# Near scores of the second attention in f16 halves, and an earlier signal for part of the last gathers

## The reference, cut to what matters

```
I = jnp.where(local[None], jnp.inf, I)
_, idx = jax.lax.top_k(I, kk)                       # kk = 96: 64 near, 32 chosen
...
scores = (jnp.einsum('bhld,bhlkd->bhlk', q_c, k_c) + jnp.einsum('bhld,blkd->bhlk', q_r, key_r)) * scale
attn = jax.nn.softmax(scores.astype(jnp.float32), axis=-1)
out = jnp.einsum('bhlk,bhlkd->bhld', attn, v)
```

## Time and profile before

| | us |
|---|---|
| median of 3 runs | 2271.33 |
| lowest, highest | 2270.91, 2275.74 |
| the profiled execution, its own time | 2271.51 |
| its span, first to last instruction | 2269.9 |
| PE, DVE, ACT, POOL busy in the span | 2103.8, 1787.5, 1732.0, 1830.0 |

### The profile page before, as it was taken

How to read it: one execution, slowest core, us unless ns; L and a number is a source line. 1 busy time by engine, 2 the same in 40 slices (tenths; PEclk the granted TensorE clock), 3 DMA queues, 4 the chain that set the end, 5 groups by cost and what they waited for, 6 DMA issues and landing times. The chain is left out here.

```text
span 2269.9 us, 56900 instructions
## 1 busy us (share of the span) xinstructions
PE 2103.8 (93%) x22674; PEld 1261.6 (56%) x22674; DVE 1787.5 (79%) x3457; ACT 1732.0 (76%) x3507; POOL 1830.0 (81%) x1239
## 2 busy tenths in 40 slices
PE   5899999999999999999999979977989889987888
PEld 1466666666666666666666646642445444444444
DVE  7788888888888888888888558978878896887314
ACT  5898898898989988989989935657567775775543
POOL 4899999999999999999999935627777777777720
PEclk9999999999999999999999989978599997998779
DMA  4000000000000000000000000111211111111101
GB/s 152 1 2 2 2 2 2 2 2 2 2 2 2 2 2 2 2 2 2 2 2 2 2 15 23 39 40 27 52 37 32 39 37 34 38 31 36 38 9 37
DMA packets 44688, 43.19 MB, mean 19 GB/s; under 512 B 21312, under 2 KB 33424, under 8 KB 44176
## 3 DMA queue, kind: packets, MB, share of 16 engines
q1 hardware_dynamic: 28560, 23.35, 3.6%
q0 software_dynamic: 15872, 16.28, 3.2%
HBM read 33.83 MB, written 1.57 MB: 16 GB/s over the span
## 5 line engine op out<-in xcount | busy, mean ns | idle before, releaser
L380 POOL TENSOR_TENSOR probs_lo<-probs,probs_hi 128x1024 f16<-128x1024 f32 x512 | 1076.9, 2130 | 42.9 <-ACT probs L430 42.4
L494 DVE TENSOR_REDUCE part_max<-aux 128x1 f32<-128x512 f32 x1024 | 677.6, 686 | 91.2 <-PE aux L568 86.8
L429 ACT ACTIVATE probs_hi<-scores 128x512 f16<-128x512 f32 x1024 | 630.2, 615 | 134.6 <-PE scores L601 117.8
L430 ACT ACTIVATE probs<-scores 128x512 f32<-128x512 f32 x1024 | 636.6, 622 | 0.0
L1617 POOL DMA_INDIRECT far<-key_table,placeT x456 | 452.2, 992 | 142.9 <-issue 138.7
L617 PE MATMUL acc<-v,probs_hi 128*128 128x65 f16 x4096 | 451.1, 193 | 2.3 <-POOL probs_lo L380 2.3
L619 PE MATMUL acc<-v,probs_hi 128*128 128x64 f16 x4096 | 452.2, 195 | 0.0
L621 PE MATMUL acc<-v,probs_lo 128*128 128x65 f16 x4096 | 450.6, 192 | 0.0
L617 PEld LDWEIGHTS acc<-v,probs_hi 128*128 128x128 f16 x4096 | 382.5, 96 | 82.6 <-POOL probs_lo L380 2.5
L619 PEld LDWEIGHTS acc<-v,probs_hi 128*128 128x128 f16 x4096 | 380.0, 97 | 75.5
L568 PE MATMUL aux<-k_a,q_a 128*128 128x512 f16 x1024 | 392.1, 383 | 5.2 <-DVE roped L480 2.1
(11 more groups left out here) (329 smaller groups left out, 3939.7 us busy)
## 6 DMA issues: line engine op xcount, KB each, us to landing
far<-key_table,placeT POOLq DMA_INDIRECT x496, 2.4
qT<-qT SPq DMA_DIRECT2D x16, 256.0 KB
e_w<-in_e_w SPq DMA_DIRECT2D x48, 64.0 KB, 1.9
x<-in_x SPq DMA_DIRECT2D x4, 256.0 KB, 3.8
cos<-in_cos SPq DMA_DIRECT2D x1, 1024.0 KB, 6.8
sin<-in_sin SPq DMA_DIRECT2D x1, 1024.0 KB, 8.8
e_w<-in_e_w SPq DMA_DIRECT2D x2, 512.0 KB, 4.0
out<-x SPq DMA_DIRECT2D x4, 256.0 KB, 2.7
```

The lines of the kernel that those rows point to most:

```text
L380: pool.tensor_tensor(probs_lo[:, slot], probs[:, wide], probs_hi[:, slot], ALU.subtract).then_inc(low_ready, 1)
L429: act.activation(probs_hi[:, slot, i], bank, ACT.Exp, scale=float(DH0) ** -0.5)
L430: act.activation(probs[:, wide, i], bank, ACT.Exp, scale=float(DH0) ** -0.5).then_inc(probs_ready, 1)
L494: dve.tensor_reduce(part_max[g % 2][:, n % QT, n // QT:n // QT + 1], bank, AX.X, ALU.max).then_inc(aux_free, 1)
```

## The change

It has two parts.

**Near scores in f16.** The near keys are kept as an f16 high part on all 128 partitions (the same 64 rows twice, `near_hi`) and an f16 low part on 64 (`near_lo`). For that each near job makes four f32 matmuls with the identity more, which put the second copy on the upper partitions, and DVE subtracts the high part after ACT's copy. The queries for the near keys are kept as high part over low part on 128 partitions (`near_qT`); ACT writes the high part and DVE the low part, with one subtraction for each of "q" 2 and 3 in each tile. The turn bank is then free when DVE is done and not when ACT is. The score is one f16 matmul of 128 partitions (high and low queries with high keys) and one of 64 (high queries with low keys), 256 columns each, in place of the f32 one. The far queries keep their form, in a tensor of their own.

**The last tile's gathers.** Its gathers 16 to 31 are signalled on two semaphores: 16 to 23 and 24 to 31. Its second "keys" item becomes two, each with half the width, the second one two slots later. Pair 2 of that tile waits for the first, pair 3 for the second. Other tiles keep their two halves.

```diff
-        by_vector = lambda kind, i: kind in ("ki", "qi")
+        by_vector = lambda kind, i: kind in ("ki", "qi", "near")
...
-                        "near": lambda: [(near[:, P + i * CH:P + (i + 1) * CH], src[0:KW, :])],
+                        "near": lambda: [(near_hi[:, P + i * CH:P + (i + 1) * CH], src[:])],
...
-                dve.memset(near[:, 0:P], 0.0).then_inc(near_ready, 1)
+                own.mark(dve.memset(near_hi[:, 0:P], 0.0))
+                dve.memset(near_lo[:, 0:P], 0.0).then_inc(near_ready, 1)
...
+                    elif kind == "near":
+                        cols = slice(P + i * CH, P + (i + 1) * CH)
+                        dve.wait_ge(hi_ready, low_no[kind, i])
+                        dve.tensor_tensor(near_lo[:, cols], src[0:KW, :], near_hi[0:KW, cols], ALU.subtract
+                                          ).then_inc(low_free, 1)
...
                         for j in range(4):
-                            ins = pe.transpose(b[0:KW, j * P:(j + 1) * P], near_key[:, 4 * i + j, :], ident[:])
+                            pe.transpose(b[0:KW, j * P:(j + 1) * P], near_key[:, 4 * i + j, :], ident[:])
+                        for j in range(4):
+                            ins = mm(b[KW:2 * KW, j * P:(j + 1) * P], near_key[:, 4 * i + j, :], ident[:])
...
+def key_parts(t):
+    return [(0, 16), (16, 24), (24, 32)] if t == LAST else [(0, 16), (16, 32)] if t else [(0, 16)]
...
-                        ins = act.activation(qT[t % 2][0:KW, 1 - i // 2, :, :, half].rearrange("k i a h -> k h a i"),
-                                             src[0:KW, :].rearrange("k (h a i) -> k h a i", h=4, a=4), ACT.Copy)
+                        dst = (near_qT if i // 2 else far_qT)[t % 2][0:KW, :, :, half].rearrange("k i a h -> k h a i")
+                        ins = act.activation(dst, src[0:KW, :].rearrange("k (h a i) -> k h a i", h=4, a=4), ACT.Copy)
+                        if i // 2:
+                            ins.then_inc(q_rounded, 1)
+                            return
...
+                    elif kind == "q" and i >= 2:
...
+                        dve.wait_ge(q_rounded, split_no[kind, t, i])
+                        dve.tensor_tensor(low, src, high, ALU.subtract).then_inc(q_split, 1)
...
+                    elif before in split_no:
+                        pe.wait_ge(q_split, split_no[before])
...
-                    if kind == "far" and i % 2 == 0:
-                        pe.wait_ge(keys_ready, keys_no(t, i // 2))
+                    if kind == "far":
+                        pe.wait_ge(keys_ready, keys_no(t, part_of_pair(t, i)))
...
-                    pe.matmul(b[:, 0:WIN], qT[t % 2][0:KW, 0, 4 * g:4 * g + 4].rearrange("k i a h -> k (i a h)"),
-                              near[:, t * P:t * P + WIN], start=False, stop=False, skip_group_check=True)
+                    window = slice(t * P, t * P + WIN)
+                    pe.matmul(b[:, 0:WIN], near_qT[t % 2][:, 4 * g:4 * g + 4].rearrange("k i a h -> k (i a h)"),
+                              near_hi[:, window], start=False, stop=False, skip_group_check=True)
+                    pe.matmul(b[:, 0:WIN], near_qT[t % 2][0:KW, 4 * g:4 * g + 4].rearrange("k i a h -> k (i a h)"),
+                              near_lo[:, window], start=False, stop=False, skip_group_check=True)
```

More of the change, by code:

```diff
@@ L1137, in projections1 @@
              "u_ready", "ln_ready", "near_ready", "hi_ready", "low_free", "mu_ready"))
-        rows, QN, near, nout, qi, ki_hi, ki_lo = (
-            keep[n] for n in ("rows", "queries", "near_keys", "nout", "qi", "ki_hi", "ki_lo"))
+        rows, QN, near_hi, near_lo, nout, qi, ki_hi, ki_lo = (
+            keep[n] for n in ("rows", "queries", "near_hi", "near_lo", "nout", "qi", "ki_hi", "ki_lo"))
         loads = [(keep["idx_w"], "idx_w"), (keep["cap0"], "cap0"), (keep["cap"], "cap"), (cos_k, "cos_k"), (sin_k, "sin_k"),
@@ L1498, in selected_schedule @@
     ahead = j + 2
-    work += [("keys", ahead // NG, ahead % NG // HALF)] if ahead % HALF == 0 and 0 <= ahead < NT * NG and ahead != HALF else []
+    work += [("keys", ahead // NG, n) for n, (lo, hi) in enumerate(key_parts(ahead // NG))
+             if 4 * (ahead % NG) == lo] if 0 <= ahead < NT * NG else []
     return work
@@ L1526, in gather_list, with part_of_pair, landed, keys_no @@
     return [(t, i) for t in range(NT) for i in range(gathers(t))]
[L1529 to L1536, removed]
+LAST = NT - 1
+def key_parts(t):
+    return [(0, 16), (16, 24), (24, 32)] if t == LAST else [(0, 16), (16, 32)] if t else [(0, 16)]
+def part_of_pair(t, pair):
+    return next(n for n, (lo, hi) in enumerate(key_parts(t)) if lo <= 8 * pair % gathers(t) < hi)
+def landed(t, part):
+    full = 256 * (t // RING + (0 if t % RING == 0 and part else 1))
+    return full - 128 if t == LAST and part == 1 else 128 if part == 2 else full
+def keys_no(t, part):
+    return 2 * t + part if t else 1
 def index_chunks(t):
@@ L1548, in selected_attention @@
         sb, ps, sem = allocators(nc, ctx)
-        rows, QN, near, nout, ctxT, qi, ki_hi, ki_lo, mask = (
-            keep[n] for n in ("rows", "queries", "near_keys", "nout", "ctxT", "qi", "ki_hi", "ki_lo", "mask"))
+        rows, QN, near_hi, near_lo, nout, qi, ki_hi, ki_lo, mask = (
+            keep[n] for n in ("rows", "queries", "near_hi", "near_lo", "nout", "qi", "ki_hi", "ki_lo", "mask"))
         space, ahead = keep["space"], keep["ahead"]
@@ L1582, in selected_attention @@
         turn_no = {w: n + 1 for n, w in enumerate(order)}
-        free_no = {w: n + 1 for n, w in enumerate(w for w in order if w[0] != "y")}
+        near_query = lambda w: w[0] == "q" and w[2] >= 2
+        free_no = {w: n + 1 for n, w in enumerate(w for w in order if w[0] != "y" and not near_query(w))}
+        split_no = {w: n + 1 for n, w in enumerate(filter(near_query, order))}
         idx_no = {w: n + 1 for n, w in enumerate(w for w in schedule if w[0] == "idx")}
@@ L1812, in _ @@
                                           ).then_inc(shift_ready, 1)
+                    elif kind == "q" and i >= 2:
+                        half = slice(4 * (i % 2), 4 * (i % 2) + 4)
+                        low, high = (near_qT[t % 2][p, :, :, half].rearrange("k i a h -> k h a i")
+                                     for p in (slice(KW, 2 * KW), slice(0, KW)))
+                        src = turn[turn_no[kind, t, i] % 2][0:KW, :].rearrange("k (h a i) -> k h a i", h=4, a=4)
+                        dve.wait_ge(q_rounded, split_no[kind, t, i])
+                        dve.tensor_tensor(low, src, high, ALU.subtract).then_inc(q_split, 1)
                     elif kind == "y":
@@ L1875, in scores @@
                         half = slice(KW * (i % 2), KW * (i % 2) + KW)
-                        queries, keys = qT[t % 2][half, 1, i], farT[half, g // 2 % 2, i % 8 // 2, :]
+                        queries, keys = far_qT[t % 2][half, i], farT[half, g // 2 % 2, i % 8 // 2, :]
                         ins = pe.matmul(b[32 * j:32 * j + 32, WIN:SC], queries.rearrange("k a h -> k (a h)"), keys,
```

36 lines of the change are left out of this document (21 added, 15 removed).

## The result

| | before | after |
|---|---|---|
| median | 2272.83 us (6 runs) | 2367.41 us (6 runs) |
| ratio | | 1.0409, 95% interval 1.0398 to 1.042 |
| profiled execution: its time, its span | 2271.51, 2269.9 | 2366.97, 2365.4 |
| PE, DVE, ACT, POOL busy in the span | 2103.8, 1787.5, 1732.0, 1830.0 | 2133.0, 1866.0, 1777.6, 1825.0 |

The change makes the kernel 95 us slower. The forecast was 2270.4, in a range up to 2276.5: wrong. Every engine but POOL has more busy time, though 26 to 64 us of PE work were to go.

A forecast was written before the change was run, and what follows sets the result against it. POOL's gather stream (its start, its length, what follows the last key) was taken as the bound; from 2271.5, -0.7 at the last tile (4.1 shift included) and -0.4 behind it gave 2270.4 us, range 2264 to 2276.5.

The forecast's parts named there:

- Part 3: Near scores: f16 matmul steps of 0.21 us, -1.3 us up to pair 2, -0.4 after; slack covers DVE's 32 subtractions.
- the third: Rival: query subtractions slow POOL (2290 or 2273 us) or hold consumers over 4.5 us a tile; chance 0.03.
- Part 1: End of the first block: extra near matmuls, copy and subtraction delay POOL's stream by 4.1 us, bounds +3.3 and +9.8.
- The rival of a doubled cost in front: First block at PE's lower clock: shift 9.8 us and not 4.1, total 2274 to 2276 us; chance 0.05.
- three signs of being wrong: POOL's stream starting within 2 us of 1581, lasting over 595 us, or last-pair-to-third-block time changing by over 3 us.
- Part 2: POOL's gather stream in the second block: new subtractions slow no gather, so it keeps 589.9 us; other bound 22 us.
- The waits of the stream have room: Tile 4's first gather starts 14.0 us after the sums of tile 0 that it needs; both ends move together.
- Part 4: Last tile's gathers split: pair 3 from 0.8 us later to 2.2 earlier, -0.7 taken, the 4.1 shift included.
- That the split does nothing: Rival at the last tile: PE and not the keys sets pair 2, total 2274 us; chance 0.10.
- the prediction's branch of full clock: Last tile with PE at full clock: pair 2 at 2174, pair 3 waits for its keys until 2178.9, 2.2 us earlier.
- The clock of the tail: Rival from 2163 to 2211 us: PE's low-clock stretches fall differently, 2 to 5 us go, 2265 to 2267; chance 0.20.
- The middle counts after all: Rival: PE is the bound in the middle, so 26 us come off, total 2245 us; chance 0.02.

The follow-up runs named there:

- e5: The changed kernel with ACT's copy and DVE's subtraction both written in runs of four f16, PSUM read with strides: 2271.61 us, ratio 0.9995.
- e8: The changed kernel without DVE's subtractions (low part of the queries zero, ACT frees the turn bank), ACT's copy still strided: 2277.66 us, ratio 1.0013.
- e7: The changed kernel with only ACT's copy in runs of four f16, DVE's subtractions still strided: 2292.82 us, ratio 1.0091.
- e10: The changed kernel with only DVE's subtractions in runs of four f16, ACT's copy still strided: 2297.39 us, ratio 1.0107.
- e6: The kernel before with only the split of the last tile's gathers, near scores still f32: 2268.75 us, ratio 0.9986.
- e11: e5's kernel with the near jobs put among the last qi jobs of the first block: 2270.95 us, ratio 0.999.
- e12: e6's kernel with the near jobs put among the last qi jobs of the first block: 2269.54 us, ratio 0.9987.
- e1: The kernel before with only the split of the last gathers, while the chip ran the kernel before at 2765.32: 2765.57 us, ratio 1.0002.
- e4: The changed kernel with copy and subtraction in runs of four f16, while the chip ran the kernel before at 2765.32: 2746.96 us, ratio 0.9919.

## Why the prediction was wrong, point by point

**The step that failed is in Part 3:** "DVE gets 32 subtractions, 0.69 each (up to 1.1 if the strided output costs as on ACT), 22 to 35 us over 590; ... the 58.7 us of slack cover it." Both the price and the cover were wrong. The 0.69 is the row of L1344, which has the type and shape of the new instruction but writes without gaps; the 1.1 is ACT's strided copy, which writes f32. The new one writes f16 and with gaps, which no row of before did, and costs 2.38. That ACT's copy would also change, from f32 to f16 at the same strides, I did not price at all: it went from 1.06 to 2.38. My upper bound was not one: each of the two rows lacked one of the two properties.

**Why the cover was gone.** From the end of the sums of tile 0 to that of tile 15 (last a_ctx), the consumers' own work is that time less their waits for gathers (their waits for each other are in it):

| kernel (all in us) | ACT, DVE form | sums of tile 0 end | sums of tile 15 end | waits for gathers | own work |
|---|---|---|---|---|---|
| before | f32, none | 1661.5 | 2211.4 | 58.7 | 491.2 |
| e5 | runs, runs | 1662.2 | 2211.6 | 72.8 | 476.6 |
| e8 | single, none | 1669.1 | 2222.7 | 1.9 | 551.7 |
| e7 | runs, single | 1673.8 | 2233.6 | 0 | 559.8 |
| e10 | single, runs | 1672.9 | 2236.7 | 0 | 563.7 |
| after | single, single | 1679.6 | 2308.1 | 0 | 628.5 |

The ends in the last row come from these two lines of PE's timeline:

```profile
1677.66 1.91 PE L1940 MATMUL a_ctx<-a_probsT,far 128*32 128x32 f32 x32
...
2306.16 1.91 PE L1940 MATMUL a_ctx<-a_probsT,far 128*32 128x32 f32 x32
```

The four kernels with the subtraction show how the two costs meet. Against e5, e7 has 83.2 us more work and tile 0 ends 11.6 later; e10 has 87.1 more and 10.7 later. Both times the 72.8 us of e5's slack swallow most of it, and the end moves by 22.0 and 25.1 us. With both slow forms the work grows by 151.9, less than the sum of 170.3, and tile 0 ends 17.4 later; less the same 72.8, the end moves by 96.5. So the two costs nearly add up as work. They seem to multiply in the time (+95 against +20 and +24) because the slack can be spent once. e8's row is of its slowest execution (2282.75, the median is 2277.66), so its end is late for it.

Part of this work is PE at its lower clock: the granted clock from 1700 to 2000 us is 0.93 before, 0.92 in e5, 0.88 in e8 and e10, 0.84 in e7 and 0.76 after. How it follows from what PE does there these rows don't tell: e7 has more busy time of PE than e10 (259.3 against 249.9 us) and the lower clock. How much of the 137 us by which after exceeds before is the clock, the runs don't separate.

**The rival that came true** is the third: "If they hold the consumers by over 58.7 / 13 = 4.5 us a tile, the gather stream stops being the bound." Its mechanism and its threshold were right. By the last column, over 15 tiles, e8 has 4.0 us a tile more than before and still waits for one gather; e7 has 4.6, e10 4.8 and after 9.2, and they wait for none. From sums to sums (tiles 2 to 10) a tile took 36.3 us before and 44.9 after, longer than the 41.5 us that its gathers take, so the sums also hold POOL. It had 0.03 with POOL's part, and "the rows speak against both" was the same mis-priced row a second time. e7 with 39.1, e8 with 39.2 and e10 with 38.7 stay under the 41.5: their gathers come back to back, and they lose 24 us at most.

**Part 1 (first block +4.1) was nearly right.** The near fills took about as long as expected (starts in PE's timeline after):

```profile
1574.98 0.63 PE L1421 MATMUL a_bank<-ident,far 128*64 128x128 f32 x4
1575.54 1.09 PE L1388 MATMUL a_bank<-ident,far 128*64 128x128 f32 x8
1576.56 0.63 PE L1421 MATMUL a_bank<-ident,far 128*64 128x128 f32 x4
```

A fill takes 1.58 us (1574.98 to 1576.56), 1.42 were predicted. POOL waited 10.0 us instead of 4.2, "over 8" was the mark. But its stream began at 1582.05, only 0.9 later than before, because in this execution DVE's last softplus instruction of the block, which the change does not touch, started 3.65 us earlier (1568.75 against 1572.40). From the start of that instruction to POOL's first gather it is 8.76 and 8.77 us without the new fills (before, e6), and 13.30 in each of after, e5, e7, e8 and e10: **+4.5**. The rival of a doubled cost in front fell with it.

The prediction named three signs of being wrong. Two came: a start within 2 us of 1581 (1582.05, by the chance of that execution) and a stream of over 595 us (647.9). The time from the last pair's transposes to the third block stayed (34.0 against 34.1).

**Part 2 (gathers not slowed) was right in its mechanism, and its zero was a little too low.** 52 gathers of the changed kernel overlap L1852 and nothing else of DVE's; they took 0.944 us on average, the undisturbed value of the earlier trace rows. The mean of all is 982 ns. This trace agrees with the rule of the Trainium skill ("GPSIMD Engine Reference", Specifications) that the prediction cites: with one input in PSUM even a 2.38 us instruction slows no gather. Yet the four kernels with the subtractions in which the sums don't hold POOL have streams of 593.5 (e5), 595.6 (e7), 595.4 (e10) and 595.9 us (e11), and the four without them 589.9 (before), 590.4 (e6), 591.2 (e8) and 589.0 (e12): 4.9 us on average (one execution of each), for which the prediction had nothing. As the gathers beside the subtractions alone aren't slowed, it may come from which other instructions of DVE the gathers meet; that is argued and not shown. What failed in this part is also the sentence "The waits of the stream have room", 14.0 us at tile 4. It was the room at the consumers' old pace; after, tile 4 itself waits 6.57 us.

**Part 3, the step of the scores, was right:** the two f16 matmuls and the next instruction start at 1841.74, 1841.94 and 1842.15 in the changed kernel, steps of 0.20 and 0.21.

```profile
1841.74 0.27 PE L1915 MATMUL a_score<-near_hi,near_qT 128*128 128x256 f16 x1
1841.94 0.28 PE L1917 MATMUL a_score<-near_lo,near_qT 64*128 64x256 f16 x1
1842.15 0.42 PE L1923 MATMUL a_score<-farT,far_qT 64*32 64x128 f32 x8
```

The gain goes where it was said to: in e5, own work is 14.6 us less than before and the waits for gathers 14.1 us more. The end doesn't move.

**Part 4 (the split) was right in its size.** Without part 1's shift my figures give it 5.2 less the 1.7 of the shorter scores, 3.5; e6 measured 3.2, of a 95% interval from 0.9 to 5.5. The half rotation takes 1.28 us (1.3 predicted). That the split does nothing lies outside this interval.

**What the forecast of 2270.4 described was e5**, at 2271.61. How near it came is partly luck. In the profiled executions the third block starts 0.7 us later in e5 than before: the first block's longer end adds 4.5 (4.1 predicted), the stream 3.6 (nothing), the earlier start of this execution takes 2.9, and from the last gather to the third block it is 39.7 us against 44.2, so the split and the shorter scores give 4.5 (5.2). e6 has 40.2 there, so the split is most of that, and the scores are worth 0.5 and not 1.7.

**"The clock of the tail"**, the likeliest of the rivals (0.20), is not settled. From 2163 to 2211 the clock was low for 27 us before and for 20 in e5 (from 2180.0, 2193.6 and 2203.8, 6.8 each), and in e5 PE reached pair 3 at 2180.31, just behind the last half rotation's end at 2180.16, as the prediction's branch of full clock has it. The runs don't separate what the clock gave there from what the split gave.

**"The middle counts after all"** fell for good: the middle got shorter by 15 us in e5 at no gain.

Open: which share of the consumers' growth is PE's clock, which of the tail's gain; why the stream is some 5 us longer with the subtractions; and what the waits of e1 to e4 were.

## What to carry to other kernels

Price a changed write by a row that has both its type and its pattern. If no row has both, there is no upper bound to be had from the rows with one of them, nor from the two together: on ACT f16 without gaps took 0.58, f32 with gaps 1.06, and f16 with gaps 2.38. Measure the form in a small run first. Price the copy whose type changes as well as the new instruction. When a 16-bit tensor must be stored in another order than it comes, put the loops so that the destination is written in runs and let the source take the strides: reordering the loops of one copy and one subtraction was worth 96 us here (2367.41 to 2271.61). A slack (here the 58.7 us that consumers wait for gathers) covers the sum of all that is added, instructions and waits, and has to be compared with that sum, engine by engine in the order in which they wait for each other.

## What the runs showed of the hardware that was not expected

- A copy or subtraction of 64 x 512 that writes f16 values one by one with gaps takes 2.34 to 2.40 us (medians) on ACT and on DVE alike, 4.6 ns for each value of a partition (2.38 / 512), 36 or 64 bytes apart. The f32 copy on ACT with the same order took 1.06.
- The same in runs of four f16 (8 bytes) takes 0.59 on ACT and 0.68 on DVE, no more than without gaps (0.58 and 0.68), though PSUM is then read with strides. Runs of two weren't tried.
- Reading single f16 values with gaps as a second input costs DVE 1.01 instead of 0.68.
- For some time one chip ran the kernel before 22% longer, with waits of up to 29.2 us on DVE and 67.7 us on ACT (e1) that no engine, queue or transfer of the trace releases. Why is open.
